# Context loads of a cross-attention stage issued from two queues instead of one, in two pieces instead of three

## Chip, cores and metric

The kernel runs on one core of one Trainium2 chip. The metric is the device time of one execution in microseconds (us). A core has five engines that take their instructions in order, each from its own stream: TensorE (PE), VectorE (DVE), ScalarE (ACT), GpSimd (POOL) and SyncE (SP). Transfers between HBM and SBUF are issued by an instruction of one of these streams, and 16 DMA engines carry them out.

## What is computed

A perceiver layer in float32: cross-attention of 64 latent rows against 1601 context rows for each of 8 batches, then causal self-attention with projections, then a gated low-rank feed-forward. The change touches only the first of the three, the cross-attention:

```python
def _L0_xattn_ref(query, key):                    # (8, 64, 2048), (8, 1601, 2048)
    a = jnp.einsum('bqd,bkd->bqk', query, key)
    e = jax.nn.softmax(a, axis=-1)
    return jnp.einsum('bqk,bkd->bqd', e, key)

x = x + _L0_xattn_ref(_layernorm(x, axis=-1), ctx_4096)
x = x + _L0_attn_ref(_layernorm(x, axis=-1), w_q, w_k, w_v, w_o)
x = x + _L0_ffn_ref(_layernorm(x, axis=-1), A_w, B_w, Wq_w, keys)
```

The same context rows serve as keys and as values, so each of them is loaded once.

## The kernel before

**Tiling.** A batch's 1601 keys are taken in two halves, a half is a stage (16 stages, `s`), and a stage has two sides (`a`), each a unit of keys (`u`, 32 units). A unit of an even stage has 13 blocks of 32 keys, one of an odd stage 12 blocks; the one key that is left over is loaded by itself. The tile `raw` (`xa_raw` in the profile) has five places for units. In it the 2048 columns of a key are folded: quadrant `i`, which is partitions 32i to 32i+31, holds columns 512i to 512i+511 of all keys, 32 keys by 512 columns per block. A block of one quadrant is 65,536 bytes, a unit of 13 blocks 3.41 MB, one of 12 blocks 3.15 MB. Within a quadrant the blocks are rotated by `i`, so that a piece can need two transfers where it wraps around (`piece_runs`, line 70).

**Stages.** For each of 16 chunks of 128 columns DVE transposes the keys of both units into one of five slots of `kt` (lines 520 and 524) and PE multiplies them with the queries (L622). The first chunk of a stage waits until all pieces of both its units have landed (line 512). PE runs the first three chunks of stage s+1 ahead of the rest of stage s; DVE transposes the first four chunks of stage s+1 ahead of the maximum of stage s (L533 to L538). Then ACT takes the exponentials of stage s (L369), PE transposes them (L642), and the values follow (L666, 13 steps `j` for each quadrant and side). "V" is used below for the time at which the values of a stage start.

**Refill.** The values of stage s free the places of its two units. Side 0's place takes unit 2s+5, the second unit of stage s+2, and side 1's takes unit 2s+6, the first of stage s+3. `PIECES` (line 45) cuts a unit into pieces of 5, 4 and 4 blocks (of an odd stage 5, 4 and 3); `pv_done` counts when the values of a piece are through, and `products` (line 280) waits on it. All loads are issued by SP in `load_unit_piece` (lines 297 to 310), in the order side 0 with its three pieces, then side 1 with its three, and each piece quadrant by quadrant in the order 0, 2, 1, 3. At the start SP loads the first tile of x (1 MB, all 128 partitions), then units 0 to 4 with the second tile of x after unit 2.

**ACT.** ACT issues no transfers. At the start it normalizes the first rows (L355), and PE turns them into queries, which ACT moves (L362), before any score can run. In an even stage ACT moves the products out of PSUM once the values are through (`evacuate`, L411). In an odd stage it first sends eight scaled parts through the three slots of `tmp` (`first_half_moved`, L403), each added by POOL (L474), and then eight more from PSUM (L415); the exponentials of the next stage come behind these in its stream.

Of the kernel before, what the change touches and what calls it, by code (L numbers as in the profile page):

```python
# [12 lines left out]
P = 128  # L13
# [19 lines left out]
HALVES, SIDES = 2, 2  # L33
STAGES = HALVES * B
SQ = 32
UNIT = 13
UNITS = SIDES * STAGES
PLACES = 5
BLOCKS = [UNIT, UNIT - 1]
COLS = [SQ * n for n in BLOCKS]  # L40
KEY0 = [0, SIDES * COLS[0]]
LEFT_KEY = LK - 1
assert SIDES * (COLS[0] + COLS[1]) == LEFT_KEY
SIDE_COLS = SQ * UNIT
PIECES = (0, 5, 9, UNIT)
NPIECE = len(PIECES) - 1
LEFT_BLOCK = UNIT - 1
QUADRANTS = P // SQ
WRAP = SQ * (QUADRANTS - 1)
LEFT_AT = COLS[1] + WRAP  # L50
QUAD_ORDER = (0, 2, 1, 3)
CHUNKS_ALL = DC * STAGES
KT_SLOTS = 5
LEAD = 3
# [4 lines left out]
A_OPS, B_OPS = 8, 8  # L59
# [5 lines left out]
def place(u):  # L65

    return (u + 2) % PLACES


def piece_runs(x, g, i):  # L70

    n = BLOCKS[x]
    j0, j1 = PIECES[g] + i, min(PIECES[g + 1], n) + i
    return [(a, b) for a, b in ((j0, min(j1, n)), (max(j0, n) - n, j1 - n)) if a < b]


def has_left(u):

    return u // SIDES % HALVES == 1 and u % SIDES == 0
# [93 lines left out]
def cross_attention(nc, stack, x_rows, ctx, x1, x1_norm, ps, ident, ident_ready, x1_tiles, x1_ahead, row_bn,  # L173
# [5 lines left out]
    def sb(name, shape, dt=F32):  # L179
        size = 4  # L180
        for n in shape[1:]:
            size *= n
        t = nc.alloc_sbuf_tensor_at(name, shape, dt, offset=here[0])
        here[0] += (size + 31) // 32 * 32
        return t

    def sem(name):
        return stack.enter_context(nc.semaphore(name))

    raw = sb("xa_raw", [P, PLACES * UNIT, 512])  # L190
# [29 lines left out]
    raw_in = [[sem(f"xa_raw_in{p}{g}") for g in range(NPIECE)] for p in range(PLACES)]  # L220
    left_clear = sem("xa_left_clear")
# [32 lines left out]
    def column(c):  # L254
        return slice(c * 512, (c + 1) * 512)

    def side(a):
        return slice(a * LQ, (a + 1) * LQ)

    def quadrant(i):  # L260
        return slice(i * SQ, (i + 1) * SQ)

    def own(b):
        return side(b % 2)

    def other(b):
        return side(1 - b % 2)
# [7 lines left out]
    def both(eng, n):  # L275

        for a in range(SIDES):
            eng.wait_ge(kt_used[a], n)

    def products(eng, s, g=NPIECE - 1, sides=range(SIDES)):  # L280

        for i in range(QUADRANTS):
            for a in sides:
                eng.wait_ge(pv_done[i][a], NPIECE * s + g + 1)

    def tmp_no(b, k):

        return BATCH_OPS * b + k

    def tmp_slot(b, k):  # L290
        return tmp[own(b), tmp_no(b, k) % TMP, :]

    def part_of(b, k):
        return own(b) if k % 2 == 0 else other(b)

    def cross_sync(sp, aside):
        def load_unit_piece(u, g):
            s, a = divmod(u, SIDES)
            b, x = divmod(s, HALVES)
            at = UNIT * place(u)  # L300
            for i in QUAD_ORDER:
                for j0, j1 in piece_runs(x, g, i):
                    k0 = KEY0[x] + a * COLS[x] + SQ * j0
                    src = ctx[b, k0:k0 + SQ * (j1 - j0), i * 512:(i + 1) * 512].rearrange("(k c) n -> c k n", c=SQ)
                    sp.dma_start(raw[quadrant(i), at + j0:at + j1, :], src).then_inc(raw_in[place(u)][g], 16)  # L305
            if g == NPIECE - 1 and has_left(u):
                if u == 2:
                    sp.wait_ge(left_clear, 1)
                left = ctx[b, LEFT_KEY, :].rearrange("(i n) -> i n", i=QUADRANTS)
                sp.dma_start(raw[0:P:SQ, at + LEFT_BLOCK, :], left).then_inc(raw_in[place(u)][g], 16)  # L310

        def load_rows(t):
            sp.dma_start(xs[t % 2][:], x_rows[t * P:(t + 1) * P, :]).then_inc(x_in[t % 2], 16)

        load_rows(0)
        for u in range(PLACES):
            for g in range(NPIECE):
                load_unit_piece(u, g)
            if u == 2:
                load_rows(1)  # L320
        for s in range(STAGES - 1):
            if s >= 5 and (s - 5) % 4 == 0:
                t = (s - 5) // 4
                sp.wait_ge(out_norm, t + 1)
                sp.dma_start(x1_norm[t * P:(t + 1) * P, :], xs[t % 2][:]).then_inc(norm_stored, 16)
            for a in range(SIDES):
                u = SIDES * s + a + PLACES
                for g in range(NPIECE):
                    if u < UNITS:
                        products(sp, s, g, [a])  # L330
                        load_unit_piece(u, g)
                    if (a, g) == (0, 0) and s >= 4 and s % 4 == 0:
                        t = s // 4 - 1
                        sp.wait_ge(pool_op, BATCH_OPS * (2 * t + 2))
                        sp.dma_start(x1[t * P:(t + 1) * P, :], xs[t % 2][:]).then_inc(x1_stored, 16)
                if a == 0 and s >= 5 and (s - 5) % 4 == 0 and s < 10:
                    sp.wait_ge(norm_stored, 16 * ((s - 5) // 4 + 1))
                    load_rows((s - 5) // 4 + 2)
            if s == STAGES - 3:
                products(sp, s)  # L340
                aside(sp, 0)
        products(sp, STAGES - 2)
        sp.wait_ge(pool_op, BATCH_OPS * (B - 1))
        sp.dma_start(x1_tiles[RT - 1][0:LQ, :], xs[1][0:LQ, :]).then_inc(sixth_in, 16)
        sp.wait_ge(norm_stored, 16 * TILES_OUT)
        for r in range(2):
            sp.dma_start(x1_ahead[r][:], x1_norm[r * P:(r + 1) * P, :]).then_inc(ahead_in[r], 16)
        aside(sp, 1)
        both(sp, CHUNKS_ALL)
        sp.dma_start(x1_ahead[2][:], x1_norm[2 * P:3 * P, :]).then_inc(ahead_in[2], 16)  # L350

    def cross_scalar(act, aside):
        def normalize_rows(t):
            act.wait_ge(ln_ready, t + 1)
            act.activation(xn[:].rearrange("p (c i r) -> p i c r", i=QUADRANTS, r=SQ),  # L355
                           xs[t % 2][:].rearrange("p (i c r) -> p i c r", i=QUADRANTS, r=SQ), ACT.Identity,
                           bias=rs[:, 4:5], scale=rs[:, 0:1]).then_inc(xn_ready, 1)

        def queries_out(b):
            for k in range(2):  # L360
                act.wait_ge(q_done, 2 * b + k + 1)
                act.activation(q_t[:, 8 * k:8 * k + 8, own(b)], ps[:, Q_BANKS[k], :].rearrange("p (c q) -> p c q", q=LQ),  # L362
                               ACT.Copy).then_inc(q_out, 1)
# [31 lines left out]
        def slot_free(n):  # L395
            if n >= TMP:
                act.wait_ge(pool_op, n - TMP + 1)

        def first_half_moved(b):
            act.wait_ge(ga_ready, b + 1)  # L400
            for k in range(A_OPS):
                slot_free(tmp_no(b, k))
                act.activation(tmp_slot(b, k), acc[part_of(b, k), column(k // 2)], ACT.Identity,  # L403
                               scale=g_a[part_of(b, k), :]).then_inc(tmp_in, 1)

        def evacuate(s):
            b, x = divmod(s, HALVES)
            products(act, s)
            for i in range(QUADRANTS):
                if x == 0:  # L410
                    act.activation(acc[:, column(i)], ps[:, i, :], ACT.Copy).then_inc(pv_out, 1)  # L411
                    continue
                for k in (A_OPS + 2 * i, A_OPS + 2 * i + 1):
                    slot_free(tmp_no(b, k))
                    act.activation(tmp_slot(b, k), ps[part_of(b, k), i, :], ACT.Identity,  # L415
                                   scale=g_b[part_of(b, k), :]).then_inc(tmp_in, 1)

        def last_moved():
            b = B - 1
            products(act, STAGES - 1)  # L420
            for i in range(QUADRANTS):
                if i < TMP:
                    slot_free(tmp_no(b, A_OPS + i))
                else:
                    act.wait_ge(finished, i - TMP + 1)
                act.activation(tmp_slot(b, A_OPS + i), ps[other(b), i, :], ACT.Identity,
                               scale=g_b[other(b), :]).then_inc(tmp_in, 1)

        normalize_rows(0)
        queries_out(0)  # L430
        for s in range(STAGES):
            b, x = divmod(s, HALVES)
# [161 lines left out]
    def cross_tensor(pe):  # L594
# [58 lines left out]
        def values(s):  # L653
            x = s % HALVES
            for j in range(UNIT):
# [3 lines left out]
                for i in range(QUADRANTS):  # L659
                    if j == 0 and s:  # L660
                        bank_free(s - 1, i)
                    for a in range(1 if left else SIDES):
# [3 lines left out]
                        ins = pe.matmul(ps[side(a), i, :], e_t[rows, j, side(a)], raw[rows, at, :], start=j == 0, stop=last)  # L666
                        if last or j + 1 in PIECES[1:-1]:
                            ins.then_inc(pv_done[i][a], 1)
# [14 lines left out]

    over = Over([p for ps_i in pv_done for p in ps_i], NPIECE * STAGES, finished, ahead_in, x1_stored, last_done)
    return over, (cross_sync, cross_scalar, cross_vector, cross_tensor, cross_gpsimd)


# [1323 lines left out]
```

## Time and profile before

| | us |
|---|---|
| median of 3 runs | 1615.15 (1615.14 to 1617.04) |
| the profiled execution | 1612.68 |
| its span, first to last instruction | 1610.9 |
| cross-attention, up to the end of its last values | about 550 |

The profile is one execution. Busy times are per engine, and a stretch of the trace can be asked for by itself. A wait is put down to what ended it. "DMA share" is the mean busy share of the 16 DMA engines (overlapping packets let it go over 1), GB/s is what they moved.

### The profile page before, as it was taken

Reading aid. Unit: us, or ns where it says so; the run is one execution under the profiler, and the core shown is the slowest. Engines: PE = TensorE matmul, PEld = TensorE weight load, DVE = VectorE, ACT = ScalarE, POOL = GpSimd, SP = SyncE. Lnnn points to the kernel's source line nnn. Section 1 sums busy time; section 2 is a strip of 40 time slices with the busy share of each in tenths; the row PEclk is TensorE's granted clock in tenths of the full one; section 3 lists DMA queues with packets and bytes.
Section 4 is the critical chain, followed back from the end, with each engine's and each line's share of the span. In section 5 each row is a group of like instructions: output and inputs, shape, how many; then the busy total and the mean of one; then the engine's idle time right before and its main releaser. Section 6 shows DMA issues by size and latency. Waiting matters only on the chain.

```text
span 1610.9 us, 24088 instructions
## 1 busy us (share of the span) xinstructions
PE 1478.6 (92%) x9593; PEld 1044.2 (65%) x9593; DVE 777.1 (48%) x1095; ACT 505.8 (31%) x698; POOL 625.3 (39%) x282
## 2 busy tenths in 40 slices
PE   1698988888889699999999999999999999999999
PEld 0233333333333388888888888888888888878777
DVE  2456646647655320446544644644465440357323
ACT  1032433433433422332423423323323332222221
POOL 0031422413405324366466564663663663430000
PEclk9899999999899799999999999999999999999999
DMA  9999899989985423233133233323331343230023
GB/s 233 247 216 227 203 255 255 216 252 254 226 238 123 139 102 108 79 105 105 56 106 98 78 104 104 102 85 99 104 104 55 106 152 105 79 105 1 29 76 131
DMA packets 182222, 219.96 MB, mean 137 GB/s; under 512 B 9488, under 2 KB 107792, under 8 KB 179504
## 3 DMA queue, kind: packets, MB, share of 16 engines
q1 hardware_dynamic: 182144, 218.87, 50.1%
q8 instruction: 55, 0.90, 0.3%
q14 instruction: 23, 0.19, 0.0%
HBM read 207.82 MB, written 10.49 MB: 136 GB/s over the span
## 4 chain that ended last, share of the span: by engine, by line
PE 76%; DMA 8%; DVE 6%; SPq 5%; issue 2%; ACT 2%; DVEq 0%; POOL 0%; ACTq 0%
PE ps L729 15%; PE ps L731 14%; PE ps L730 14%; PE ps L666 11%; DMA xa_raw<-in_ctx 8%; SPq L305 5%; PE ps L1769 5%; PE ps L1771 5%; PE ps L1770 5%; DVE xa_kt L520 2%; PE ps L642 2%; PE ps L1709 2%; PE ps L1862 1%; DVE xa_kt L524 1%; PE ps L1734 1%
## 5 line engine op out<-in xcount | busy, mean ns | idle before, releaser
L729 PE MATMUL ps<-h_hi,w_hi 128*128 128x512 f32 x800 | 315.4, 394 | 1.2 <-DVE h_lo L1425 1.1
L731 PE MATMUL ps<-h_hi,w_lo 128*128 128x512 f32 x800 | 311.7, 390 | 0.0
L730 PE MATMUL ps<-h_lo,w_hi 128*128 128x512 f32 x800 | 311.5, 389 | 0.0
L1157 POOL TENSOR_TENSOR w_lo<-raw,w_hi 128x2048 fp32r<-128x2048 f32 (+1 forms) x52 | 212.7, 4095 | 254.4 <-ACT w_hi L1222 213.8
L474 POOL TENSOR_TENSOR xa_x<-xa_x,xa_tmp 64x512 f32<-64x512 f32 x120 | 150.3, 1269 | 360.0 <-ACT xa_tmp L403 348.1
L622 PE MATMUL ps<-xa_kt,xa_q_t 128*64 128x416 f32 (+2 forms) x1024 | 211.1, 557 | 78.7 <-DVE xa_kt L520 56.4
L520 DVE STREAM_TRANSPOSE xa_kt<-xa_raw 128x832 f32<-128x832 f32 (+1 forms) x208 | 193.9, 995 | 158.4 <-PE ps L622 102.9
L622 PEld LDWEIGHTS ps<-xa_kt,xa_q_t 128*64 128x64 f32 x1024 | 71.8, 146 | 208.1 <-issue 134.5
L666 PE MATMUL ps<-xa_raw,xa_e_t 32*64 32x512 f32 (+1 forms) x3264 | 184.1, 593 | 0.0
L729 PEld LDWEIGHTS ps<-h_hi,w_hi 128*128 128x128 f32 x800 | 150.2, 188 | 36.4 <-issue 6.4
L1513 DVE TENSOR_TENSOR rows<-rows,ps 128x512 f32<-128x512 f32 x168 | 115.5, 688 | 116.3 <-PE ps L1771 116.3
L731 PEld LDWEIGHTS ps<-h_hi,w_lo 128*128 128x128 f32 x800 | 150.2, 188 | 31.7
L730 PEld LDWEIGHTS ps<-h_lo,w_hi 128*128 128x128 f32 x800 | 150.3, 188 | 29.9
L1163 POOL TENSOR_TENSOR w_lo<-wo_t_sum,w_hi 128x1024 fp32r<-128x1024 f32 x48 | 115.0, 2407 | 68.7 <-ACT w_hi L1251 68.7
L666 PEld LDWEIGHTS ps<-xa_raw,xa_e_t 32*64 32x64 f32 (+1 forms) x3264 | 72.1, 133 | 100.5 <-issue 97.1
L1769 PE MATMUL ps<-w_hi,wo_a_hi 128*128 128x512 f32 x336 | 131.3, 391 | 0.0
L1770 PE MATMUL ps<-w_lo,wo_a_hi 128*128 128x512 f32 x336 | 130.8, 389 | 0.0
L1163 POOL TENSOR_TENSOR w_lo<-raw,w_hi 128x1024 fp32r<-128x1024 f32 x36 | 97.4, 2720 | 63.8 <-ACT w_hi L1251 63.8
L1299 ACT ACTIVATE sa_q_t<-ps 128x512 f32<-128x512 f32 x32 | 19.1, 598 | 263.7 <-PE ps L731 263.7
L1771 PE MATMUL ps<-w_hi,wo_a_lo_o 128*128 128x512 f32 x192 | 74.8, 389 | 0.0
L1493 DVE TENSOR_TENSOR wo_t_sum<-raw 128x1024 f32<-128x1024 f32 x12 | 37.2, 3102 | 74.4 <-DMA raw<-in_L_attn_w_o 74.4
L1770 PEld LDWEIGHTS ps<-w_lo,wo_a_hi 128*128 128x128 f32 x336 | 63.1, 188 | 12.9
(222 smaller groups left out, 1894.3 us busy)
## 6 DMA issues: line engine op xcount, KB each, us to landing
xa_raw<-in_ctx SPq DMA_DIRECT2D x128, 320.0 KB, 8.5
xa_raw<-in_ctx SPq DMA_DIRECT2D x144, 256.0 KB, 11.0
raw<-in_L_attn_w_q SPq DMA_DIRECT2D x32, 1024.0 KB, 5.9
raw<-in_L_attn_w_o SPq DMA_DIRECT2D x30, 1024.0 KB, 5.0
xa_raw<-in_ctx SPq DMA_DIRECT2D x64, 192.0 KB
xa_raw<-in_ctx SPq DMA_DIRECT2D x64, 128.0 KB
raw<-in_L_attn_w_k SPq DMA_DIRECT2D x8, 1024.0 KB, 5.2
raw<-in_L_attn_w_v SPq DMA_DIRECT2D x8, 1024.0 KB, 5.2
```

Of the source, the lines that this page charges most:

```text
L474: pool.tensor_tensor(x[own(b), column(i)], x[own(b), column(i)], tmp_slot(b, k), ALU.add).then_inc(pool_op, 1)
L520: dve.transpose(slot[:, 0:SQ * k].rearrange("p (k r) -> p k r", r=SQ), raw[:, at[0]:at[0] + k, part]).then_inc(kt_ready, 1)
L622: pe.matmul(s_bank(s)[side(a), 0:cols], q_t[:, c, own(b)], slot[:, a * SIDE_COLS:a * SIDE_COLS + cols], start=c == 0, stop=c == DC - 1).th ...
L666: ins = pe.matmul(ps[side(a), i, :], e_t[rows, j, side(a)], raw[rows, at, :], start=j == 0, stop=last)
L729: pe.matmul(out, hi, mov_hi, start=first, stop=False)
L730: pe.matmul(out, hi, mov_lo, start=False, stop=False)
L731: return pe.matmul(out, lo, mov_hi, start=False, stop=last)
L1157: pool.tensor_tensor(w_lo[:, n % 2, part], raw[:, n % 2, part], w_hi[:, n % 2, part].bitcast(F32), ALU.subtract).then_inc(w_lo_done, 1)
L1163: pool.tensor_tensor(half_slot(w_lo, p), half_source(p), half_slot(w_hi, p).bitcast(F32), ALU.subtract).then_inc(w_lo_done, 1)
L1769: pe.matmul(out, st_hi, hi[:, wc], start=first and k == 0, stop=False, skip_group_check=True)
L1770: pe.matmul(out, st_hi, lo[:, wc], start=False, stop=False, skip_group_check=True)
L1771: ins = pe.matmul(out, st_lo, hi[:, wc], start=False, stop=k == 1, skip_group_check=True)
```

## The change

Quadrants 0 and 1 of every piece are issued by SP as before, quadrants 2 and 3 by ACT. A unit comes in two pieces (7 and 6 blocks; of an odd stage 7 and 5) instead of three. The order of SP's loads by side and piece is as before, with two quadrants in each. ACT issues all its loads of units 0 to 4 before its first instruction; in stage s it then issues piece 0 of both sides before piece 1 of both sides: in an even stage both right ahead of `evacuate`, in an odd stage piece 0 between the fourth and the fifth part of `first_half_moved` and piece 1 ahead of `evacuate`. What each piece waits for is the same counter as before. A unit's loads go from 15 transfers (4, 4 and 7; 14 in an odd stage) to 11 (4 and 7), of which ACT issues 6 (2 and 4). The left-over key's transfer stays with SP.

```diff
-PIECES = (0, 5, 9, UNIT)
+PIECES = (0, 7, UNIT)
-QUAD_ORDER = (0, 2, 1, 3)
+QUEUE_QUADS = ((0, 1), (2, 3))
...
+    def load_unit_piece(eng, queue, u, g):
...
+        for i in QUEUE_QUADS[queue]:
+            for j0, j1 in piece_runs(x, g, i):
...
+                eng.dma_start(raw[quadrant(i), at + j0:at + j1, :], src).then_inc(raw_in[place(u)][g], 16)
+        if queue == 0 and g == NPIECE - 1 and has_left(u):
...
                     if u < UNITS:
                         products(sp, s, g, [a])
-                        load_unit_piece(u, g)
+                        load_unit_piece(sp, 0, u, g)
...
+        def refill(s, g):
+            for a in range(SIDES):
+                u = SIDES * s + a + PLACES
+                if u < UNITS:
+                    products(act, s, g, [a])
+                    load_unit_piece(act, 1, u, g)
+
         def first_half_moved(b):
             act.wait_ge(ga_ready, b + 1)
             for k in range(A_OPS):
+                if k == A_OPS // 2:
+                    refill(HALVES * b + 1, 0)
                 slot_free(tmp_no(b, k))
...
         def evacuate(s):
             b, x = divmod(s, HALVES)
+            for g in range(x, NPIECE):
+                refill(s, g)
             products(act, s)
...
+        for u in range(PLACES):
+            for g in range(NPIECE):
+                load_unit_piece(act, 1, u, g)
         normalize_rows(0)
         queries_out(0)
```

## Rows read from the trace of the kernel before

**Rows 1.** Busy time by stretch; columns are named in the first line
```profile
core 0: us, PE busy (x) PEld busy (x) DVE busy (x) ACT busy (x) POOL busy (x), PEclk, DMA share, GB/s
0.00:72.00 72.00, 22.20 (x113) 9.80 (x121) 27.37 (x49) 6.64 (x10) 2.60 (x11) 0.91 1.02 242
72.00:505.00 433.00, 376.87 (x4046) 157.06 (x4031) 264.44 (x468) 159.89 (x308) 140.22 (x112) 0.93 0.94 230
562.00:1611.00 1049.00, 1037.56 (x4937) 857.79 (x4935) 466.33 (x547) 316.97 (x342) 463.37 (x149) 1.00 0.29 91
```

**Rows 2.** Waits of DVE, 0 to 510 us: us in total, times, longest
```profile
DVE xa_kt L520 <- DMA xa_raw<-in_ctx: 55.5, 12, 23.5
DVE xa_kt L524 <- DMA xa_raw<-in_ctx: 20.4, 3, 14.4
```

**Rows 3.** Chain that ended last, stages 7 and 8: start, us, what
```profile
288.74 11.44 PE ps L666 x200
...
302.49 7.96 DMA xa_raw<-in_ctx
...
315.17 0.70 ACT xa_expo L369 x2
...
317.82 11.57 PE ps L666 x207
```

**Rows 4.** DMA rate by stretch, columns as in rows 1
```profile
12.00:45.00 33.00, 10.49 (x52) 5.30 (x54) 9.74 (x11) 3.09 (x3) 0.00 (x0) 1.00 1.06 237
336.00:349.00 13.00, 7.82 (x30) 2.10 (x28) 8.49 (x13) 2.69 (x6) 0.00 (x0) 0.74 1.06 290
598.00:604.00 6.00, 6.00 (x28) 4.96 (x27) 0.00 (x0) 0.00 (x0) 4.59 (x1) 1.00 1.02 429
```

**Rows 5.** Timeline of DVE: start, us, what, [idle before, and releaser]
```profile
35.26 14.94 DVE L520 STREAM_TRANSPOSE xa_kt<-xa_raw 128x832 f32<-128x832 f32 x16 [23.49 <-DMA xa_raw<-in_ctx]
64.56 3.93 DVE L524 STREAM_TRANSPOSE xa_kt<-xa_raw 128x416 f32<-128x416 f32 x8 [14.36 <-DMA xa_raw<-in_ctx]
...
310.78 3.69 DVE L520 STREAM_TRANSPOSE xa_kt<-xa_raw 128x800 f32<-128x800 f32 x4 [2.17 <-DMA xa_raw<-in_ctx]
...
342.95 3.82 DVE L520 STREAM_TRANSPOSE xa_kt<-xa_raw 128x832 f32<-128x832 f32 x4 [4.43 <-DMA xa_raw<-in_ctx]
```

**Rows 6.** SP's issues of context loads: ns min/median/max, first and last start
```profile
L305 SPq DMA_DIRECT2D xa_raw<-in_ctx x464: 311/432/3266, 1.2 to 489.3; - x155
```

**Rows 7.** Chain that ended last, 8 to 66 us: start, us, what
```profile
9.88 0.44 SPq L305
...
10.36 1.12 SPq L305
...
50.15 14.09 DMA xa_raw<-in_ctx
```

**Rows 8.** Timeline of ACT, first queries
```profile
11.80 2.09 ACT L355 ACTIVATE xa_xn<-xa_x,xa_rs 128x2048 f32<-128x2048 f32 x1 [9.77 <-DVE xa_rs L492]
...
16.01 0.60 ACT L362 ACTIVATE xa_q_t<-ps 128x512 f32<-128x512 f32 x1 [0.26 <-PE ps L605]
```

**Rows 9.** Timeline of SP, first loads of stage 7's refill
```profile
293.52 2.96 SPq L305 DMA_DIRECT2D xa_raw<-in_ctx  x3
```

**Rows 10.** Timelines of ACT and POOL, odd stage 7
```profile
292.43 2.95 ACT L403 ACTIVATE xa_tmp<-xa_acc,xa_g_a 64x512 f32<-64x512 f32 x4 [0.35 <-DVE xa_g_a L560]
295.94 0.72 ACT L403 ACTIVATE xa_tmp<-xa_acc,xa_g_a 64x512 f32<-64x512 f32 x1 [0.56 <-POOL xa_x L474]
...
301.32 0.68 ACT L415 ACTIVATE xa_tmp<-ps,xa_g_b 64x512 f32<-64x512 f32 x1 [0.78 <-POOL xa_x L474]
...
310.43 0.68 ACT L415 ACTIVATE xa_tmp<-ps,xa_g_b 64x512 f32<-64x512 f32 x1 [0.54 <-POOL xa_x L474]
...
293.23 21.23 POOL L474 TENSOR_TENSOR xa_x<-xa_x,xa_tmp 64x512 f32<-64x512 f32 x16 [39.47 <-ACT xa_tmp L403]
```

**Rows 11.** Timeline of PE, first scores and the values of stage 8
```profile
36.45 14.72 PE L622 MATMUL ps<-xa_kt,xa_q_t 128*64 128x416 f32 x64 [20.48 <-DVE xa_kt L520]
...
317.75 11.41 PE L666 MATMUL ps<-xa_raw,xa_e_t 32*64 32x512 f32 x208
```

More of the change, by code:

```diff
@@ L294, in part_of @@
         return own(b) if k % 2 == 0 else other(b)
-    def cross_sync(sp, aside):
[L297 to L310, printed above, removed]
+    def load_unit_piece(eng, queue, u, g):
+        s, a = divmod(u, SIDES)
+        b, x = divmod(s, HALVES)
+        at = UNIT * place(u)
+        for i in QUEUE_QUADS[queue]:
+            for j0, j1 in piece_runs(x, g, i):
+                k0 = KEY0[x] + a * COLS[x] + SQ * j0
+                src = ctx[b, k0:k0 + SQ * (j1 - j0), i * 512:(i + 1) * 512].rearrange("(k c) n -> c k n", c=SQ)
+                eng.dma_start(raw[quadrant(i), at + j0:at + j1, :], src).then_inc(raw_in[place(u)][g], 16)
+        if queue == 0 and g == NPIECE - 1 and has_left(u):
+            if u == 2:
+                eng.wait_ge(left_clear, 1)
+            left = ctx[b, LEFT_KEY, :].rearrange("(i n) -> i n", i=QUADRANTS)
+            eng.dma_start(raw[0:P:SQ, at + LEFT_BLOCK, :], left).then_inc(raw_in[place(u)][g], 16)
+    def cross_sync(sp, aside):
         def load_rows(t):
@@ L330, in cross_sync @@
                         products(sp, s, g, [a])
-                        load_unit_piece(u, g)
+                        load_unit_piece(sp, 0, u, g)
                     if (a, g) == (0, 0) and s >= 4 and s % 4 == 0:
```

## The prediction

> **What bounds the kernel now.** I read the stretches first. After 562 us PE is busy 1037.6 of 1049 us, and the change touches nothing there; from 72 to 505 us PE is busy 377 of 433 us while the DMA engines stand at a share of 0.94, and in the first 72 us PE has 22 us of work and the share is 1.02 [rows 1]. So whatever can be won lies before 505 us. Next come DVE's waits, since DVE is first to touch the loaded keys: 55.5 + 20.4 = 75.9 us for context loads in 15 waits [rows 2]. Two are the start: 23.49 us until units 0 and 1 are there and 14.36 us until units 2 and 3 are [rows 5]. That leaves 38.0 us in 13 waits, 2.93 us each, one in nearly every stage. The chain shows how such a wait closes a loop: the values of stage 7 end at 300.2, the chain goes on through a load that lands 10 us later, then through transposes, exponentials and the values of stage 8 at 317.8 [rows 3]. The load is that of unit 2s+5: its last piece is set free by the values of stage s, and DVE must transpose four chunks of it before the maximum of stage s+1.
>
> Then the rate. Pure context loads move 237 GB/s at a DMA share of 1.06, weight loads into all 128 partitions 429 GB/s at a share of 1.02 [rows 4]. The engines are as busy, yet move 0.55 of the bytes, so what a context load lacks is not an engine. For 13 us of stage 8 the same quadrant loads in the same order ran at 290 GB/s [rows 4]. My reading, an inference: a transfer into one quadrant reaches about half of the way into SBUF, engines in step crowd on that half, and they do better when they are out of step.
>
> The Trainium skill would explain this ("SBUF — State Buffer", section "Door 1: The DMA port swizzle"): partitions 0 to 63 are reached through eight of sixteen ports and 64 to 127 through the other eight. The rows agree with half of 429 being near 237; no row shows a port. By that rule two queues, one on either half, could together approach 429.
>
> **The rate after.** No row has two queues. The low end is 237 (they share one way), the high end 429. The 290 shows that it can exceed 237 without a second queue. I take 400: nearer to 429, because each engine then always has one transfer for either half to go on with, and less than 429, because pairs of engines can still meet on one. That is 200 GB/s per queue.
>
> **Start, from 0 us.** Units 0 to 3 (2 x 3.41 + 2 x 3.15 MB) and two tiles of x (2.1 MB) are 15.2 MB. At 237 they take 64.1 us, and indeed DVE goes on at 64.56 [rows 5]. At 400 they take 38.0 us, with 1.5 us for first issue and landing 39.5.
> Now ACT stands in the way. It must have issued 30 transfers before the first normalization, and an issue blocks when too much is outstanding: SP's go at 0.44 us until 10.36 us and then at about a microsecond [rows 7], up to 3.27 us at worst [rows 6]. The load issued at 50.15 us landed 14.09 us later [rows 7], so about 14.09 x 0.237 = 3.3 MB can be outstanding. ACT's half of units 0 to 4 is 8.27 MB; 4.93 MB must be gone, 24.7 us at 200 GB/s, with 1.2 us for the start 25.9. From there to queries takes 16.61 - 11.80 = 4.8 us [rows 8], so scores can begin at 30.7, before 36.45 as now [rows 11]. Five chunks are transposed by then; eleven more at 14.94/16 = 0.934 us [rows 5], and 0.7 for the first score, reach 41.7 us. That is later than the 39.5 of the data, so it decides: the first transposes of stage 1 move from 64.56 to 41.7, **22.9 us won**. If the second queue only shared 237, ACT would reach them at 41.6 + 1.2 + 4.8 + 11.0 = 58.6, still under 64.56: nothing won or lost.
>
> **Steady stages.** DVE has finished the chunks before and looks for the new unit at 310.78 - 2.17 = 308.6, V + 19.9, in odd stage 7, and at 342.95 - 4.43 = 338.5, V + 20.7, in even stage 8 [rows 3, 5]. When does it land?
> - Today SP issues stage 7's first piece at 293.52, V + 4.8 [rows 9]; 48 blocks (3.15 MB) at 237 take 13.3 us, to 306.8; DVE starts at 310.78. So 4.0 us are for issue, landing and lag among engines. I take 3.0 after (lag should shrink with the rate), between 2 and 4.
> - After, a first piece is free at 7/13 of the values' 11.4 us [rows 11]: V + 6.2 rather than 4.8, the price of two pieces. In an odd stage ACT comes to it after four parts, at 295.38, V + 6.7 [rows 10]. ACT's queue then has piece 0 of side 0, piece 0 of side 1, which is not urgent, and only behind it piece 1 of side 0: 2 x (7 + 7 + 6) = 40 blocks, 2.62 MB, in an even stage, 38 blocks, 2.49 MB, in an odd one. SP sends piece 1 of side 0 second, so ACT's queue decides.
> - Even: 6.2 + 13.1 + 3.0 = V + 22.3, a wait of 1.6 us. Odd: 6.7 + 12.45 + 3.0 = V + 22.15, 2.25 us. The mean of 1.9 against 2.93 gives 1.0 x 13 = **13 us**. The one stage that does not wait today may lose up to 2 us; I leave that to the range.
>
> **ACT's added work.** One issue costs 0.43 us unblocked [rows 6]; ACT is another engine, so 0.3 to 1.1 us [rows 6, 7] bound it, and I take SP's median with 0.04 us between [rows 7]. Per stage it gets 12 issues, 5.6 us. In an odd stage the first four (1.9 us) fall between 295.4 and 297.3, while POOL, at 21.23/16 = 1.33 us a part, still has parts until 298.5: hidden. The eight ahead of `evacuate` (3.8 us) run from about 300.6 to 304.4, POOL has parts until 303.9, so the L415 parts end near 312.3 instead of 311.1 [rows 10]; the exponentials come at 315.17 today [rows 3], at about 315.2 after. Hidden, with some 3 us of cover. What waits behind these issues in ACT's stream are the L415 parts, which free PSUM for the next values, and those exponentials. In an even stage evacuation starts 3.8 us later and has until V + 25. SP loses about two thirds of its issues; its 0.43 us steps in the chain go, but they stood before a queue that was full, so I give them nothing. Its wait for piece 1 of side 0 now holds back side 1's first piece, which is not needed for a stage.
>
> **Sum.** 1612.7 - 22.9 - 13 = 1576.8 by the profiled execution, which is 2.5 us below the median; against the median, 1579.
>
> **Rivals.**
> - *The rate does not rise.* Then the loop is longer, not shorter: a piece later, and behind a piece that is not urgent. At 237: even 6.2 + 22.1 + 3.0 = V + 31.3, odd 30.7, waits of 10.6 and 10.8 us; (10.7 - 2.93) x 13 = 101, with 10 for the stage without a wait 111: 1726 us. At 290 waits are near 6.8 us, 56 us lost with the same stage, and the start wins 64.56 - 53.9 = 10.7: 1660 us, slower. It turns at about 340 GB/s: waits of 4.2 us, 16 us lost, 18 won. For it: the order 0, 2, 1, 3 already alternates the halves in one queue and gets only 237. Against: the 290.
> The Trainium skill sides with this rival ("DMA: Bandwidth & Descriptors", section "Rules for kernel authors"): two transfers to disjoint partition halves serialize on the same engines, and spreading issues over engines saves issue time alone. By that rule the sum is 1726. The trace is at odds with it as far as 237 against 429 at the same DMA share goes.
> - *ACT becomes the bound.* At 1.0 us an issue, the eight ahead of `evacuate` end 4.6 us later, exponentials move to about V + 28.2 against V + 26.5 in my forecast: 1.7 x 7 = 12 us; the start gives back 5 (30 + 1.2 + 4.8 + 11 = 47 us). 1596 us.
> - *Loads are hidden altogether.* At 429, waits of 0.7 and 1.4 us: 24 + 24.6 won, 1566; all 38 + 25 us gone, 1552.
>
> **Chances.** Forecast (1560 to 1600) 0.48; hidden below that 0.07; ACT-bound 0.12, of which 0.02 within 0.2% of no change; rate too low, slower 0.28; rate near 340, no change, 0.05. About 0.2% (3 us) is what a measurement tells from no change. So faster 0.65, same 0.07, slower 0.28. The range goes from 1552 (all hidden) to 1660 (290 GB/s).
>
> **What would show it.** Right: over 340 GB/s from 12 to 35 us, first stage-1 transposes near 42 us, 13 waits of DVE near 2 us, ACT's L355 near 26 us, its odd-stage L415 parts ending before DVE has the maximum. Wrong: rates near 237 to 290 with a share still over 1, DVE waits of 7 us and more; or ACT issues of a microsecond, and exponentials that follow ACT's own work instead of DVE.

## The result: 32 us slower, at a load rate that did rise

| | before | after |
|---|---|---|
| median, us | 1615.49 | 1647.33 (1638.91 to 1648.83, 4 runs) |
| ratio | 1 | 1.0184 (95% interval 1.015 to 1.0219) |
| the profiled execution, us | 1612.68 | 1648.83 |
| its span, us | 1610.9 | 1647.0 |

Forecast were 1579 us and "faster". The time lies inside the range (1552 to 1660) only because that range reached to a case in which the loads stay near 290 GB/s; the sign is wrong. It came out slower, as the first rival said, though the rate did rise. The busy time by stretch of the changed kernel, in the columns of rows 1 (its last line answers to the first line of rows 4):

```profile
0.00:72.00 72.00, 26.67 (x233) 11.46 (x241) 28.61 (x50) 7.24 (x11) 2.60 (x11) 1.00 0.78 259
72.00:540.00 468.00, 372.41 (x3925) 154.18 (x3910) 262.25 (x464) 158.30 (x305) 140.25 (x112) 0.90 0.69 210
597.00:1647.00 1050.00, 1038.88 (x4934) 858.87 (x4932) 465.40 (x545) 316.93 (x342) 462.30 (x149) 1.00 0.29 91
12.00:45.00 33.00, 1.94 (x16) 1.78 (x16) 5.67 (x10) 4.29 (x4) 0.00 (x0) 1.00 1.05 357
```

The later layers take what they took [rows 1]. At the start the loads run at 357 GB/s instead of 237 [rows 4] with the DMA engines as busy as before. But from 72 to 540 us the DMA share has fallen from 0.94 to 0.69: the engines now stand idle for nearly a third of the stages, and the stages are still longer. Faster loads did not shorten the loop that waits for them. TensorE did not lengthen it either: it is busy for 372 us of these stages where it was 377, at a mean granted clock of 0.90 of full speed where it was 0.93.

Where the 36 us of the span are, by the start of the values of stage 0 and of stage 14 on PE. First the kernel before:

```profile
71.77 11.41 PE L666 MATMUL ps<-xa_raw,xa_e_t 32*64 32x512 f32 x208
...
505.08 11.74 PE L666 MATMUL ps<-xa_raw,xa_e_t 32*64 32x512 f32 x208
```

and the changed one:

```profile
65.24 11.41 PE L682 MATMUL ps<-xa_raw,xa_e_t 32*64 32x512 f32 x208
...
540.26 11.41 PE L682 MATMUL ps<-xa_raw,xa_e_t 32*64 32x512 f32 x208
```

The start wins 6.5 us. The fourteen stages take 475.0 us instead of 433.3, a loss of 41.7. What follows differs by 0.9 (1647.0 - 540.3 = 1106.7 against 1105.8). The loss is in DVE's waits for loads (us in total, times, longest):

```profile
DVE xa_kt L536 <- DMA xa_raw<-in_ctx: 80.1, 13, 13.3
DVE xa_kt L540 <- DMA xa_raw<-in_ctx: 15.5, 2, 8.0
```

Without the 13.3 us at the start these are 82.3 us in 14 waits, 5.9 us each, where there were 38.0 us in 13 [rows 2]: 44.3 us more, about the loss of the stages.

### The profile page after: what moved, and what is told of

Its sections match the earlier page's. It is cut to its first block, busy times and chain, and to the rows that moved or that the text cites. A ratio compares the mean times of both kernels' runs of the same rounds, so it can differ in the third digit from the quotient of the medians.

```text
span 1647.0 us, 24014 instructions
## 1 busy us (share of the span) xinstructions
PE 1480.3 (90%) x9593; PEld 1045.1 (63%) x9593; DVE 777.0 (47%) x1095; ACT 505.1 (31%) x698; POOL 624.2 (38%) x282
## 4 chain that ended last, share of the span: by engine, by line
PE 74%; DMA 11%; DVE 5%; ACTq 4%; ACT 2%; issue 2%; POOL 1%; SPq 0%; DVEq 0%; POOLq 0%
PE ps L745 14%; PE ps L747 14%; PE ps L746 14%; DMA xa_raw<-in_ctx 11%; PE ps L682 9%; PE ps L1787 5%; PE ps L1786 5%; PE ps L1785 5%; ACTq L305 4%; DVE xa_kt L536 2%; PE ps L1725 2%; PE ps L658 2%; PE ps L1878 1%; PE ps L638 1%; POOL xa_x L490 1%
## 5 line engine op out<-in xcount | busy, mean ns | idle before, releaser
L746 PE MATMUL ps<-h_lo,w_hi 128*128 128x512 f32 x800 | 312.4, 390 | 0.0
L746 PEld LDWEIGHTS ps<-h_lo,w_hi 128*128 128x128 f32 x800 | 150.9, 189 | 30.2
```

What stands on the lines that cost most here:

```text
L746: pe.matmul(out, hi, mov_lo, start=False, stop=False)
```

## What holds a stage of the changed kernel

Even stage 6, first its chain of waits (start, us, what):

```profile
268.41 11.57 PE ps L682 x207
...
282.30 12.51 DMA xa_raw<-in_ctx
...
295.10 1.06 DVE xa_kt L536
```

The awaited load was issued by ACT, as in all 14 stages. ACT's and SP's own rows in that stage (start, us, with the count of issues merged into one row):

```profile
274.92 9.76 ACTq L305 DMA_DIRECT2D xa_raw<-in_ctx  x12
285.02 2.06 ACT L424 ACTIVATE xa_acc<-ps 128x512 f32<-128x512 f32 x4 [8.97 <-issue]
...
274.90 9.76 SPq L305 DMA_DIRECT2D xa_raw<-in_ctx  x10
```

And what each queue moved (q1 is SP's, q10 ACT's; packets, MB, share of the 16 engines), first from 277 to 292 us, then the three microseconds from 282 to 285 alone:

```profile
q10 hardware_dynamic: 1387, 2.60, 62.9%
q1 hardware_dynamic: 1035, 1.96, 41.3%
...
q10 hardware_dynamic: 345, 0.66, 104.4%
q1 hardware_dynamic: 21, 0.02, 3.4%
```

V is 268.34. ACT issues at V + 6.6. Its queue moves nothing before 277, then needs until 292 for the 2.62 MB that end with the awaited piece, 0.173 MB/us, and DVE goes on at 295.10: 6.6 + 2.1 + 15.0 + 3.1 = V + 26.8. Of the 2.62 MB, 0.92 MB are the first piece of side 1, for which DVE does not wait before the next stage. Whether that order is what costs is for the experiments to say.

Stage 6 is near the mean. Counted from the DMA packets of the trace, the means of stages 0 to 12 are: issue at V + 6.6, first packet of ACT's queue at V + 8.8, 15.4 us for the 2.62 MB (of an odd stage 2.49), 0.168 MB/us, and DVE 2.5 us later, at V + 26.7. Both queues together move 320 GB/s meanwhile (302 to 354). The five stages in which SP's queue also carries a megabyte of x or of its result (4, 5, 8, 9 and 12) need 16.0 to 18.0 us, the other eight 13.8 to 15.2.

## Experiments

The kernel before was timed beside each group of runs: 1617.1 us beside e1 to e4, 1615.2 beside e5 to e8, 1614.5 beside e9 and e7b. Intervals are of the ratio to it. In the code, `...` marks what is left out.

**The order in ACT's queue (e3).**

```diff
-        def refill(s, g):
...
+        def refill(s, a, g):
+            u = SIDES * s + a + PLACES
...
-                    refill(HALVES * b + 1, 0)
+                    refill(HALVES * b + 1, 0, 0)
...
-            for g in range(x, NPIECE):
-                refill(s, g)
+            for a in range(SIDES):
+                for g in range(x if a == 0 else 0, NPIECE):
+                    refill(s, a, g)
```

> The changed kernel with one edit: ScalarE issues side 0 with both its pieces and then side 1, as SyncE does. Order theory: 26 blocks instead of 40 lie up to the end of the awaited unit, 0.92 MB less, 4.7 us at 0.195 MB/us; VectorE's 13 waits for loads fall from 5.9 us to 1.5 us, 1585 to 1595 us. Pieces theory: the last piece is set free at the same time, so under 15 us change: 1632 to 1647 us.

Both pieces of side 0 now go ahead of those of side 1. Measured: 1595.8 us, ratio 0.987 (0.984 to 0.9899), 51.5 us under the changed kernel, faster than the kernel before, and just above what the order theory gave (1585 to 1595). DVE's waits for loads in e3 (us in total, times, longest):

```profile
DVE xa_kt L535 <- DMA xa_raw<-in_ctx: 28.8, 9, 12.3
DVE xa_kt L539 <- DMA xa_raw<-in_ctx: 6.4, 2, 4.1
```

Less the 12.3 at the start they are 22.9 us in the stages instead of 82.3. The bytes of the awaited unit are through ACT's queue at V + 20.5 on the mean of stages 0 to 12, where it was V + 24.2. The two queues and the number of pieces are as in the changed kernel; the order alone carries the sign. It gave 51.5 us where the waits fell by 59.4, since something else is late next. The chain of e3 behind odd stage 1:

```profile
115.58 0.69 ACT xa_tmp L427
...
122.92 0.68 ACT xa_tmp L427
123.63 0.70 ACT xa_expo L370 x2
```

ACT's last part ends at 123.60 and the exponentials follow 0.03 us later: here they wait for ACT's own stream, which had ten issues ahead of these parts. The same stands in stages 3 and 7. It is the sign of the second rival of the prediction, once the loads were out of the way and without its price: the ten issues took 5.9 us, not 1.0 us each. What it costs is for e9 to say.

**The start (e4).**

```diff
         for u in range(PLACES):
             for g in range(NPIECE):
                 load_unit_piece(act, 1, u, g)
-        normalize_rows(0)
-        queries_out(0)
+            if u == 1:
+                normalize_rows(0)
+                queries_out(0)
```

> The changed kernel with one edit: ScalarE issues units 0 and 1, then normalizes the first rows and moves the queries, and then issues units 2 to 4. Start theory: the values of stage 0 begin near 49 us instead of 65.3, and the whole is 16 us shorter: 1631 us. Rival: the stages behind take it up, or the loads of units 2 and 3 now come later than the scores want them: under 5 us, 1642 to 1647 us.

Measured: 1633.2 us, 1.0105 (1.0071 to 1.0139), 14 us under the changed kernel. ACT in the changed kernel and then in e4:

```profile
0.75 38.40 ACTq L305 DMA_DIRECT2D xa_raw<-in_ctx  x30
39.18 1.28 ACT L356 ACT_TABLE_LOAD   x1 [39.18 <-issue]
40.47 2.09 ACT L356 ACTIVATE xa_xn<-xa_x,xa_rs 128x2048 f32<-128x2048 f32 x1
```

```profile
0.75 8.28 ACTq L305 DMA_DIRECT2D xa_raw<-in_ctx  x12
...
13.13 2.09 ACT L356 ACTIVATE xa_xn<-xa_x,xa_rs 128x2048 f32<-128x2048 f32 x1 [2.79 <-DVE xa_rs L509]
```

Thirty issues held ACT for 38.4 us, twelve took 8.3: an issue takes 0.45 us at the median, but one among the thirty took 4.85. Queries are ready 27 us sooner. The first transposes of stage 1, in the changed kernel and then in e4, where they wait for their data alone:

```profile
58.06 2.48 DVE L540 STREAM_TRANSPOSE xa_kt<-xa_raw 128x416 f32<-128x416 f32 x5
```

```profile
46.86 3.93 DVE L541 STREAM_TRANSPOSE xa_kt<-xa_raw 128x416 f32<-128x416 f32 x8 [6.11 <-DMA xa_raw<-in_ctx]
```

So what the start lost, it lost to ACT's own issues. The fourteen stages take 472.2 us in e4, 475.0 in the changed kernel: they did not take it up.

**The two parts of the change apart (e1, e2).** e1 is the changed kernel with three pieces, e2 the kernel before with two.

```diff
-PIECES = (0, 7, UNIT)          # e1
+PIECES = (0, 5, 9, UNIT)
-PIECES = (0, 5, 9, UNIT)       # e2
+PIECES = (0, 7, UNIT)
```

> The changed kernel with three pieces again (5, 4, 4 blocks), two queues kept: the queue part of the change alone. Three theories of why the changed kernel is 32 us slower. Order: ScalarE's queue sends the first piece of side 1, which nobody waits for, ahead of the last piece of side 0. Here 2 x (5+5+4+4+4) = 44 blocks lie up to the end of the awaited unit where it was 40, but the first is released 1.4 us earlier: 1647 us, give or take 10. Pieces: the later release is what costs; then about 1.4 to 1.9 us come back in each of 14 stages: 1621 to 1628 us. Start: only ScalarE's late start costs; then nothing changes: 1647 us.

> The kernel before with two pieces (7 and 6 blocks), all from SyncE: the pieces part of the change alone. Pieces theory: the loop runs from the release of the first piece at the rate of one queue, so 1.4 to 1.9 us later in each of 14 stages: 1635 to 1642 us. Order theory: pieces alone cost little, since the queue still holds the side before: 1615 to 1622 us.

Measured: e1 1663.6 us (1.0249 to 1.0316), e2 1646.1 us (1.016 to 1.0224). DVE's waits in e2:

```profile
DVE xa_kt L520 <- DMA xa_raw<-in_ctx: 80.5, 13, 25.1
DVE xa_kt L524 <- DMA xa_raw<-in_ctx: 27.0, 3, 15.9
```

Less the two at the start they are 66.5 us, 28.5 more than the 38.0 of before, and e2 is 29.0 us slower. So two pieces cost 29 us while one queue is the bound: the pieces theory had that right in sign, and expected somewhat less (1635 to 1642 us). But with two queues three pieces are not better: 46 us slower than before, 16 slower than with two. By ACT's order each more piece puts another piece of side 1 ahead of the one that is awaited. That this makes the third piece costly is argued, with e6 below in its favour: there, with the order mended, three pieces cost nothing. e1 is outside what the order theory allowed (10 us either way), on the slower side; the pieces theory wanted 1621 to 1628.

**The halves (e7, e8).** Two queues again, with the quadrants shared out otherwise.

```diff
-QUEUE_QUADS = ((0, 1), (2, 3))
+QUEUE_QUADS = ((0, 2), (1, 3))     # e7
+QUEUE_QUADS = ((0, 2), (3, 1))     # e8
```

> The changed kernel with quadrants 0 and 2 from SyncE and 1 and 3 from ScalarE. Halves theory (quadrants 0 and 1 share one half of the way into SBUF, 2 and 3 the other): both queues start in the lower half and go over to the upper one together, so they move 225 to 280 GB/s from 12 to 36 us instead of 370. Rival (two queues are faster whatever they write): 360 to 375 GB/s.

> The changed kernel with quadrants 0 and 2 from SyncE, in this order, and 3 and 1 from ScalarE. Halves theory: the queues start in opposite halves and stay so as long as they keep in step, with some loss where they drift: 300 to 375 GB/s from 12 to 36 us, well over e7_same_half. Rival (it is the pairing within a queue that counts): the same as e7_same_half.

> e7_same_half once more, for its time, since TensorE was about three times slower through the whole of that execution, the unchanged later layers included. By the rate of the first look (269 GB/s from 12 to 36 us, e8_opposite_half 245): 1690 to 1720 us, near e8_opposite_half's 1714. Rival: the rate was low only because that execution was disturbed: 355 to 375 GB/s and 1640 to 1655 us.

In e7 (4077.5 us) TensorE was slow throughout, in later layers that no edit touches too (a matmul of L746 took 829 ns instead of 390). Its time is therefore not read, only its rate, 269 GB/s; e7b is the same kernel again. Rates from 12 to 36 us, e7b and e8 in this order:

```profile
12.00:36.00 24.00, 0.00 (x0) 0.00 (x0) 3.26 (x7) 0.00 (x0) 0.00 (x0) 1.00 1.06 269
```

```profile
12.00:36.00 24.00, 0.00 (x0) 0.00 (x0) 0.60 (x3) 0.00 (x0) 0.00 (x0) 1.00 1.06 245
```

In the same stretch, before, after and in e3:

```profile
12.00:36.00 24.00, 1.94 (x16) 1.78 (x16) 0.74 (x1) 3.09 (x3) 0.00 (x0) 1.00 1.06 238
```

```profile
12.00:36.00 24.00, 0.00 (x0) 0.00 (x0) 5.67 (x10) 0.00 (x0) 0.00 (x0) 1.00 1.06 362
```

```profile
12.00:36.00 24.00, 0.00 (x0) 0.00 (x0) 5.67 (x9) 0.00 (x0) 0.00 (x0) 1.00 1.05 373
```

So two queues by themselves bring little (245 to 269 against 238): it counts that one queue writes to quadrants 0 and 1 alone and the other to 2 and 3 alone. The rival "two queues are faster whatever they write" falls, and so does that of e7b, that the first execution's rate was low only because it was disturbed. The expectation for e8 falls too: to begin in opposite halves was not enough. SP begins with a tile of x, so ACT is ahead of it, and two queues that meet in one half are slow there together; that this is why is argued, not shown. The times, of one execution each, are 1740.0 us (e7b) and 1714.1 (e8), far over the changed kernel's: the rate the change does bring is worth having. e7b is slower than its expectation allowed (1690 to 1720), and slower than e8 at a higher rate at the start; why is open.

**Together (e5, e6, e9).** e5 has the edits of e3 and e4. e6 adds three pieces. e9 is e5 with ACT's issues of side 1 behind other work: between the parts of an odd stage, and behind the evacuation of an even one. Its edit of `evacuate`, against the changed kernel:

```diff
             for g in range(x, NPIECE):
-                refill(s, g)
+                refill(s, 0, g)
...
+                    if k == A_OPS + 3:
+                        refill(s, 1, 0)
+                    if k == A_OPS + 5:
+                        refill(s, 1, 1)
+            if x == 0:
+                for g in range(NPIECE):
+                    refill(s, 1, g)
```

> The changed kernel with both edits: ScalarE takes side 0 before side 1 (1595.8 us by itself) and does the first queries after units 0 and 1 (14 us by itself). If the start and the stages are separate losses, they add: 1580 to 1584 us. Rival: with the start out of the way the stages catch up on the loads sooner, and part of the 14 us goes into waits: 1588 to 1595 us.

> As e5_both, with three pieces (5, 4, 4 blocks). If the release of the first piece still sets the loop, it comes 1.4 us earlier where VectorE still waits for loads, in some 9 stages: 6 to 12 us under e5_both. Rival: ScalarE's added issues (8 instead of 6 for each unit, 0.45 us each) delay its exponentials in odd stages, and it comes out even or up to 10 us slower than e5_both.

> As e5_both, with ScalarE's issues of side 1 moved behind work that others wait for: between the L415 parts of an odd stage, where ScalarE waits for GpSimd anyway, and behind the evacuation of an even stage. If ScalarE's issues ahead of these parts now hold the exponentials in odd stages (its last part ends and the exponentials start at once in two of the first seven), 1 to 2 us come back in seven stages: 1573 to 1580 us. Rival: side 1's later loads meet the next stage's on the way and VectorE waits instead: 1586 to 1592 us.

| | us | interval of the ratio |
|---|---|---|
| e5 | 1586.3 | 0.9789 to 0.9842 |
| e6 | 1583.7 | 0.9787 to 0.9837 |
| e9 | 1589.6 | 0.982 to 0.9893 |

e5 is 9.5 us under e3, where e4 alone gave 14: between its expectation (1580 to 1584) and the rival's (1588 to 1595). By the profiled executions the waits did not eat the rest: the values of stage 0 start 12.0 us earlier than in e3 (53.49 against 65.51), those of stage 14 13.5 us earlier, and what follows took 1108.0 us against 1104.9, for which these runs show no cause. e6 cannot be told from e5, where 6 to 12 us were expected: with the order mended the earlier release brings nothing that can be measured. e9 brings nothing either, as its rival had it (1586 to 1592). ACT no longer holds the exponentials, which wait for DVE again behind every odd stage with such issues; but DVE's waits up to 480 us are 48.4 us in it and 43.1 in e5, so what ACT no longer held up, later loads did. All three beat both kernels, e5 by some 29 us the one before.

## Why the prediction was wrong, point by point

- **The rate** rose, but not to what the sum used, least of all in the stages. I took 400 GB/s, between 237 and 429; it was 357 at the start and 394 at best, from 356 to 364 us. While the stages waited, it was 320 on average, and 0.168 MB/us in ACT's queue instead of 0.200: below the 340 GB/s (0.170 in a queue) at which the prediction itself turns to no gain. The first rival, no rise, is refuted; its warning that too low a rate makes the loop longer came true in part.
  Refuted with it is the rule of the Trainium skill that I weighed ("DMA: Bandwidth & Descriptors", section "Rules for kernel authors"), that transfers to disjoint partition halves serialize: 357 against 237 GB/s from spreading over two queues is more than saved issue time. The other page ("SBUF — State Buffer", section "Door 1: The DMA port swizzle"), by which partitions 0 to 63 have one half of the ports and 64 to 127 the other, agrees with e7 and e8, where the halves, not the queues, made the difference; no run shows a port.
- **Start, 22.9 us: the step that failed is the time at which ACT is free.** I had 25.9 us; it was 39.2. Up to 39.2 us ACT's queue had moved 5.65 MB of its 8.27, so 2.6 MB were outstanding when the last issue went through, not the 3.3 that I had from SP; and it moved them at 0.171 MB/us from 10 to 36 us, and only 0.51 MB before 8 us, while SP's queue, with the tile of x, moved 1.30, not at 0.200 from 1.2 us. That is 13.3 us. Another 3.0 came behind it: from ACT's release to the first score it took 6.2 us instead of 4.8, a table load of 1.28 among them, and the eleven chunks and the first score 12.7 instead of 11.0. Stage 1's first transposes came at 58.06 instead of 41.7. That scores would decide over data was right, and e4 shows it. Its size was missed by 16 us.
- **Stages, 13 us won: the step that failed is the time at which the awaited piece lands.** I had V + 22.3 in an even stage; stage 6 has V + 26.8. The terms of the sum: issue at V + 6.2, measured 6.6; 2.62 MB in 13.1 us at 0.200, measured 15.0 at 0.173; and 3.0 us for issue, landing and lag, measured 2.1 + 3.1 = 5.2. I let that last term shrink with the rate, from 4.0; it grew. Together 4.5 us, and the mean wait is 5.9 where I had 1.9. The wait begins where I had it (V + 20.8 in stage 6, V + 20.7 in the sum); its end is what was wrong. Over stages 0 to 12 the rate is the larger part: 15.4 us for the bytes instead of 12.8, 4.7 for issue, landing and lag instead of 3.0, 6.6 for the release instead of 6.4. The release had been worked out without the 0.4 us by which SP's issue of before already trailed it (V + 4.8, where 5/13 of 11.4 us are 4.4). By my own turning point, with 0.170 MB/us for a queue, the stages would have lost 16 us to the rate alone; the lag made it more, priced at the wrong side of what the row of before had shown. The slow rate goes with the tiles of x on SP's queue and with the stalls told below; the cause of the stalls and of the longer lag is open.
- **What I saw and did not weigh:** that ACT's queue carries a piece that is not urgent ahead of the awaited one stood in the sum, as 40 blocks, but its price stood nowhere. It was worth 51.5 us (e3). The trace of the changed kernel had a sign of it: stage 13, the last with a refill, has no side 1 to load, and DVE waits 2.07 us there, least of all stages.
- **The stage that did not wait before** (stage 5) was left to the range with up to 2 us; it waited 7.9.
- **ACT's added work** held in the stages. An issue takes 0.45 us at the median, with 0.43 assumed. POOL's gap behind the first eight parts of odd stage 7 is 1.14 us, with 1.2 worked out, and the exponentials still followed DVE there:

```profile
307.95 10.64 POOL L490 TENSOR_TENSOR xa_x<-xa_x,xa_tmp 64x512 f32<-64x512 f32 x8 [47.95 <-ACT xa_tmp L414]
319.73 10.60 POOL L490 TENSOR_TENSOR xa_x<-xa_x,xa_tmp 64x512 f32<-64x512 f32 x8 [1.14 <-ACT xa_tmp L428]
...
331.37 0.61 ACT L370 ACTIVATE xa_expo<-ps,xa_neg 128x416 f32<-128x416 f32 x1 [4.38 <-DVE xa_neg L554]
```

- **Two pieces** I had priced at 1.4 us of later release in a stage. With one queue (e2) the fourteen stages take 458.6 us instead of 433.3, 1.8 more each, and 3.1 us more go at the start, where the rate is 225 GB/s instead of 238.

## What to carry to other kernels

When loads are spread over two queues, look at what stands in each queue ahead of the transfer that somebody waits for: the time to that landing counts, not the bytes per second of the whole, and here one misplaced piece outweighed a rate half as high again. An engine that computes and also issues can be held by its own issues, here for 38.4 us, so what others need from it comes before a long run of issues. A fixed part of a measured latency should not be scaled down with a rate until a row shows that it shrinks. And a rate that two queues reach when both are kept full (357 GB/s) is not the rate of a stage in which they start, stall and share with other transfers (320).

## What the runs showed of the hardware that was not expected

- From 12 to 36 us, two queues that write to quadrants 0 and 1 and to quadrants 2 and 3 reach 359 to 376 GB/s (seven kernels); two queues that each go over both halves 245 to 269; one queue that goes over both halves 238, or 225 with two pieces (e2).
- In stage 6 of the changed kernel SP's queue moved 0.02 MB from 282 to 285 us while ACT's moved 0.66, although SP had been issuing its second pieces since 280.05. In nine of stages 0 to 12 SP's queue likewise moves at most 0.01 MB in two microseconds that start between V + 13.8 and V + 15. At the first pieces it is ACT's queue that is late: issued at 274.92, two hundredths after SP's, it moved nothing before 277, SP's 0.11 MB. Why an issued transfer waits that long beside another queue was not settled, and it is a part of the 5.2 us above.
